# Second attention's keys made behind the last expert slot, routed rows added in one block, 52 unread matmuls ahead of an attention

## What is computed

```python
x = x + tanh(g_xattn[0]) * _L0_xattn_ref(_layernorm(x), ctx, ctx, ...)          # sigmoid attention
x = x + tanh(g_ffn[0])   * _L0_ffn_ref(_layernorm(x), Wr, br, W1, b1, W2, ...)  # 8 experts, three layers, gelu
x = x + tanh(g_xattn[1]) * _L1_xattn_ref(_layernorm(x), ctx, ctx, mask, ...)    # softmax attention
x = x + tanh(g_ffn[1])   * _L1_ffn_ref(_layernorm(x), gate_w, w1, b1, ...)      # 2 experts and a shared FFN
# inside the attention: k = K @ Wk_w + Wk_b ; v = V @ Wv_w + Wv_b   with K = V = ctx
# inside the last part: return routing_output + shared
```

## Time and profile before

| | before |
|---|---|
| median of 3 runs | 883.76 us (882.13 to 883.86) |
| profiled execution | 884.19 us, of which the span of the core is 882.7 us |
| PE, DVE, ACT, POOL busy | 77%, 58%, 37%, 27% of the span |
| mean granted PE clock | 0.887 of full speed |
| stages, from the first instruction of each | sigmoid attention 0, experts 134.9, softmax attention 465.0, last part 680.1 us |

### The profile page before, as it was taken

One profiled execution on the slowest core, in us unless ns is written; L12 is line 12 of the kernel. 1 busy time (PEld: TensorE's weight loads), 2 busy tenths in 40 slices (PEclk: granted clock), 3 DMA queues, 4 the chain that ended last, 5 costly groups with the idle time before them and its releaser, 6 DMA issues. The chain is left out here.

```text
span 882.7 us, 14792 instructions
## 1 busy us (share of the span) xinstructions
PE 679.5 (77%) x4920; PEld 622.8 (71%) x4921; DVE 514.9 (58%) x1231; ACT 323.4 (37%) x546; POOL 237.1 (27%) x365
## 2 busy tenths in 40 slices
PE   3787952176899989999851666786987989999957
PEld 2456642176899988999850453575877889999947
DVE  5543226555775457744634798885554876555535
ACT  3532410444543345433423245434322523333311
POOL 8443326600000000000006165454000621110340
PEclk9897965688999999999985787987999999999978
DMA  4970002624550015660004001000001611111232
GB/s 155 395 296 1 1 0 78 247 84 151 169 175 24 24 71 196 226 232 24 24 30 138 12 1 48 1 1 1 1 1 41 240 62 48 41 34 45 60 95 71
DMA packets 21125, 78.13 MB, mean 89 GB/s; under 512 B 4193, under 2 KB 8546, under 8 KB 16898
## 3 DMA queue, kind: packets, MB, share of 16 engines
q1 hardware_dynamic: 13922, 56.05, 17.4%
q0 software_dynamic: 7168, 21.63, 8.2%
HBM read 50.94 MB, written 33.03 MB: 95 GB/s over the span
## 5 line engine op out<-in xcount | busy, mean ns | idle before, releaser
L1290 ACT ACTIVATE e_h<-psum,e_be 128x256 f32<-128x256 f32 x144 | 67.6, 474 | 148.7 <-PE psum L52 145.1
L50 PE MATMUL psum<-e_h_hi,e_w_hi 128*128 128x256 f32 x384 | 110.3, 287 | 6.2 <-DVE e_w_lo L1374 5.5
L51 PE MATMUL psum<-e_h_lo,e_w_hi 128*128 128x256 f32 x384 | 107.9, 281 | 0.0
L52 PE MATMUL psum<-e_h_hi,e_w_lo 128*128 128x256 f32 x384 | 107.8, 281 | 0.0
L1366 DVE CAST e_h_hi<-e_h 128x256 fp32r<-128x256 f32 x144 | 43.3, 301 | 89.5 <-ACT e_h L1290 89.3
L1635 ACT ACTIVATE vz<-psum,fb 128x256 f32<-128x256 f32 x112 | 52.6, 475 | 115.1 <-PE psum L52 100.3
L50 PEld LDWEIGHTS psum<-e_h_hi,e_w_hi 128*128 128x128 f32 x384 | 72.3, 188 | 9.6 <-DVE e_w_lo L1374 8.8
L51 PEld LDWEIGHTS psum<-e_h_lo,e_w_hi 128*128 128x128 f32 x384 | 72.4, 188 | 0.0
L52 PEld LDWEIGHTS psum<-e_h_hi,e_w_lo 128*128 128x128 f32 x384 | 72.4, 188 | 0.0
L50 PE MATMUL psum<-e_gT_hi,e_w_hi 128*128 128x256 f32 x192 | 56.1, 292 | 15.2 <-issue 7.3
L1368 DVE TENSOR_TENSOR e_h_lo<-e_h,e_h_hi 128x256 fp32r<-128x256 f32 x144 | 61.2, 425 | 4.9
(11 more groups left out here) (367 smaller groups left out, 2157.5 us busy)
## 6 DMA issues: line engine op xcount, KB each, us to landing
e_w_raw<-in_W SPq DMA_DIRECT2D x18, 1024.0 KB, 6.7
xs<-zeros SPq DMA_DIRECT2D x6, 1024.0 KB, 9.5
ys<-zeros SPq DMA_DIRECT2D x6, 1024.0 KB, 14.4
ys<-e_yo POOLq DMA_DIRECT2D x14, 256.0 KB, 3.1
e_xg<-xs POOLq DMA_DIRECT2D x13, 256.0 KB, 3.1
e_w_raw<-in_W SPq DMA_DIRECT2D x6, 512.0 KB, 8.1
f_w_lo<-fw SPq DMA_DIRECT2D x6, 512.0 KB, 7.6
ys<-x_norm POOLq DMA_DIRECT2D x10, 256.0 KB, 2.5
```

The costliest lines, as they stand in the source:

```text
L50: nc.tensor.matmul(out, wh, xh, start=start, stop=False)
L51: nc.tensor.matmul(out, wh, xl, start=False, stop=False)
L52: return nc.tensor.matmul(out, wl, xh, start=False, stop=stop)
L1290: nc.scalar.activation(h32[:, m % RING], ps[:, HIDDEN_BANKS[m % RING], 0:SLOT], ACT.Gelu, bias=be[:, m:m + 1]).then_inc(gelu_ok, 1)
```

## The change

1. In the sigmoid attention the last of the eight norms is refined by DVE (normalise_on_vector, moved up in the file) and applied by ACT.
2. In the experts' stage the zeros of kz_hi, kz_lo and vz are written by ACT (a copy with scale 0) and not by POOL. The keys and values are made behind the loop, in the buffers of w1_hi, w1_lo and xg. DVE makes the low parts of ctx and of the weights ahead of the last slot's bias (finish), and the rest behind it. The values use other PSUM banks.
3. The second attention opens with 52 matmuls of 512 columns on kz_hi, into a bank that is written again before anyone reads it. ACT runs q_hi(0) ahead of norm_1(1).
4. In the last part unit 6 is an ordinary shared unit. In unit 7 the splits run first, then DVE waits for the gathered rows and adds all 16 tiles in a row, then the shared result.

```diff
-            for q in range(len(NORMS)):
+            for q in range(len(NORMS) - 1):
                 pool.wait_ge(mv_ok, q + 1)
...
+                if s == B:
+                    act.wait_ge(rs_ok, len(NORMS))
+                    for i in range(TB):
+                        t = (B - 1) * TB + i
+                        last = nc.scalar.activation(k["xn"][:, t, :], k["x"][:, t, :], ACT.Identity,
+                                                    bias=ln_shift[:, len(NORMS) - 1, i:i + 1], scale=ln_rstd[:, len(NORMS) - 1, i:i + 1])
+                    last.then_inc(n2_ok, 1)
...
                 dve.wait_ge(mv_ok, q + 1)
+                if q == len(NORMS) - 1:
+                    normalise_on_vector(nc, dve, ln_mv[:, q], last_half[:], last_tmp[:], ln_rstd[:, q], ln_shift[:, q], last_step, 0).then_inc(rs_ok, 1)
...
             act.wait_ge(fb_ld, 32)
+            q_hi(0)
             norm_1(1)
-            q_hi(0)
...
+            for _ in range(52):
+                nc.tensor.matmul(ps[:, 7, :], kz_hi[:, 0, 0, 0:P], kz_hi[:, 0, 0, :], start=True, stop=True)
             input_T(0)
...
-                nc.gpsimd.memset(f32(kz_hi[:]), 0.0).then_inc(kz0, 1)
-                nc.gpsimd.memset(f32(kz_lo[:]), 0.0).then_inc(kz0, 1)
-                nc.gpsimd.memset(vz[:], 0.0).then_inc(vz0, 1)
...
+            none = k["ident"][:, None, :]
+            for t in (kz_hi, kz_lo):
+                flat = t[:].rearrange("p b c n -> p (b c n)").rearrange("p (a n) -> p a n", n=P)
+                nc.scalar.activation(flat, none.to_broadcast([P, B * C * HPC * KEYS // P, P]), ACT.Copy, scale=0.0).then_inc(kz0, 1)
...
             visits = dve.value_load(meta[0:1, E0:E0 + 1], min_val=1, max_val=E0)
+            nc.vector.tensor_reduce(odd[:], k["head_rows"][:].rearrange("p (j a) -> p a j", a=2), AX.X, ALU.add).then_inc(odd_ok, 1)
+            dve.wait_ge(ctxh_ok, 1)
...
             finish(n1, visits + 1)
+            dve.wait_ge(odd_ok, 1)
+            dve.wait_ge(kz0, 2)
...
-                sp.wait_ge(x_ok, (b + 1) * TB)
+                sp.wait_ge(x_ok, (b + 1) * TB + b // (B - 1))
...
-            for u in range(DONE + PB, UNITS - PB):
+            for u in range(DONE + PB, UNITS):
                 hidden(u - DONE + n1)
-                for t in range(HALVES):
-                    add_shared(u - DONE + n1, t, k["x"][:, u * HALVES + t, :])
...
+                if u == UNITS - 1:
+
+                    dve.wait_ge(got, 16 * NT)
+                    dve.wait_ge(y_used, (UNITS - DONE - 1 + n1) * HALVES + 2)
+                    for t in range(NT):
+                        add_routed(t).then_inc(x_ok, 1)
+                    dve.wait_ge(x_ok, NT)
                 for t in range(HALVES):
                     add_shared(u - DONE + n1, t, k["x"][:, u * HALVES + t, :])
```

More of the change, by code:

```diff
@@ L70, in normalise, with normalise_on_vector, link @@
     return nc.gpsimd.tensor_scalar(shift, shift, -1.0, None, ALU.mult), count
+def normalise_on_vector(nc, dve, mv, half, tmp, rstd, shift, step, q):
+    count = 10 * q
+    def link(ins):
+        nonlocal count
+        count += 1
+        ins.then_inc(step, 1)
+        dve.wait_ge(step, count)
+    link(nc.vector.tensor_scalar(half, mv[:, :, 1], EPS, -0.5, ALU.add, ALU.mult))
+    for _ in range(3):
+        link(nc.vector.tensor_tensor(tmp, rstd, rstd, ALU.mult))
+        link(nc.vector.tensor_tensor(tmp, tmp, half, ALU.mult))
+        link(nc.vector.scalar_tensor_tensor(out=rstd, in0=tmp, scalar=1.5, in1=rstd, op0=ALU.add, op1=ALU.mult))
+    return nc.vector.scalar_tensor_tensor(out=shift, in0=mv[:, :, 0], scalar=-1.0, in1=rstd, op0=ALU.mult, op1=ALU.mult)
 def sigmoid_attention(nc, k, io):
@@ L505, in _ @@
                     project(s)
[L508 to L523, removed]
 def softmax_attention(nc, k, io):
@@ L1308, in _ @@
             act.sem_inc(gelu_ok, RING)
[L1309 to L1320, removed]
-            for j in range(QUADS):
-                for a in range(2):
-                    r = slice(2 * HD * j, 2 * HD * (j + 1))
-                    nc.scalar.activation(of_head(kz_hi, j, a), of_rows(j), ACT.Copy, scale=odd[r, a:a + 1]).then_inc(kzh_ok, 1)
+            none = k["ident"][:, None, :]
+            for t in (kz_hi, kz_lo):
+                flat = t[:].rearrange("p b c n -> p (b c n)").rearrange("p (a n) -> p a n", n=P)
+                nc.scalar.activation(flat, none.to_broadcast([P, B * C * HPC * KEYS // P, P]), ACT.Copy, scale=0.0).then_inc(kz0, 1)
+            flat = vz[:].rearrange("p b j d -> p (b j d)").rearrange("p (a n) -> p a n", n=P)
+            nc.scalar.activation(flat, none.to_broadcast([P, B * PAIRS * 2 * HD // P, P]), ACT.Copy, scale=0.0).then_inc(vz0, 1)
             act.wait_ge(zero_ok, 1)
@@ L1345, in _ @@
                 act.end_ifs()
+            nc.scalar.activation(ctx_hi, k["ctx_raw"][:, :, :, None, :].to_broadcast([P, C, B, 2, KEYS]), ACT.Copy).then_inc(ctxh_ok, 1)
+            for w in range(2):
+                nc.scalar.activation(kw_hi[:, w], k["w_raw"][:, w], ACT.Copy).then_inc(kwh_ok, 1)
+            act.wait_ge(kp_done, 1)
+            act.wait_ge(kb_ld, 32)
+            for m in range(C):
+                last = nc.scalar.activation(kT[:, :, m, :], ps[:, 2 + m, 0:B * KEYS].rearrange("p (b n) -> p b n", b=B), ACT.Identity,
+                                            bias=bk[:, m:m + 1])
+            last.then_inc(kT_ok, 1)
+            act.wait_ge(kT_ok, 1)
+            act.wait_ge(odd_ok, 1)
+            for j in range(QUADS):
+                for a in range(2):
+                    r = slice(2 * HD * j, 2 * HD * (j + 1))
+                    nc.scalar.activation(of_head(kz_hi, j, a), of_rows(j), ACT.Copy, scale=odd[r, a:a + 1]).then_inc(kzh_ok, 1)
         @block.vector
@@ L1509, in _ @@
                 pe.end_ifs()
+            pe.wait_ge(gelu_ok, n1 * BL + RING)
+            pe.wait_ge(gl_ok, n1 + 1)
+            pe.wait_ge(ctxl_ok, 1)
+            pe.wait_ge(kwl_ok, 1)
+            for m in range(C):
+                for c in range(C):
+                    w = slice(m * P, (m + 1) * P)
+                    last = mm3(nc, ps[:, 2 + m, 0:B * KEYS], kw_hi[:, 0, c, w], kw_lo[:, 0, c, w],
+                               ctx_hi[:, c, :, 0, :], ctx_lo[:, c, :, 0, :], c == 0, c == C - 1)
+            last.then_inc(kp_done, 1)
+            pe.wait_ge(kwl_ok, 2)
+            for b in range(B):
+                for c in range(C):
+                    last = mm3(nc, ps[:, VALUE_BANKS[b], 0:D], ctx_hi[:, c, b].rearrange("p t n -> p (t n)"),
+                               ctx_lo[:, c, b].rearrange("p t n -> p (t n)"), kw_hi[:, 1, c, :], kw_lo[:, 1, c, :], c == 0, c == C - 1)
+                last.then_inc(vp_done, 1)
 def last_ffn_phase(nc, k, io, out):
@@ L1752, in _ @@
             dve.wait_ge(y_used, (UNITS - DONE + n1) * HALVES + 2)
-            dve.sem_inc(x_ok, TB)
+            dve.sem_inc(x_ok, 1)
         @block.tensor
```

82 lines of the change are left out of this document (29 added, 53 removed).

## The result

| | before | changed |
|---|---|---|
| median, the runs of the result (4 and 4) | 883.81 us (882.13 to 886.02) | 861.37 us (859.30 to 863.89) |
| ratio, 95% interval | | 0.9746 (0.9712 to 0.9780) |
| profiled execution, span | 884.19, 882.7 | 860.92, 859.4 |
| granted clock, PE busy | 0.887, 77% | 0.907, 80% |
| last part, from its first instruction to the end | 202.6 us | 188.0 us |

The prediction said 860.6. The last row is why the number must not be carried off alone: on chip 4 the changed kernel is worth nothing. The chip of the first runs is not on record.

What follows compares the result with a forecast made beforehand. The prediction took five stretches where PE waits for chains of small operations as what could move; six differences summed to -23.2 us, giving 860.6 us against the median 883.76, range 855.6 to 866.7.

Steps and rivals of the forecast that it cites:

- last norm: End of the sigmoid attention: the last norm on DVE and ACT takes 4.30 us, not POOL's 6.55; -2.3 us.
- fills leave POOL: Experts' stage: without POOL's fills a held DVE operation takes 0.17 us, not 6.95, so the scatter comes earlier; -6.8 us.
- scatter: Experts' stage: scatter pieces stretch less without keys and values made beside them; -1.6 us, bounds 0 and -2.8.
- keys behind the loop: End of the experts' stage: keys and values, formerly free under the scatter, now delay the stage's end; +6.8 us.
- opening of the softmax attention: Second attention's start: transposes at full clock and query rounded ahead of batch 1's norm bring scores sooner; -4.3 us.
- last part: Shared units 5 to 7: unit 6 follows at once, the wait for gathered rows is covered, 16 additions take 6.5; -15.0 us.
- With q_hi(0) ahead, it is rounded before DVE has ended the norm: Softmax attention's opening: q_lo(0) then follows the norm at once and scores start at 491.4; part of the -4.3 us.
- the 52 matmuls do not help: Rival, softmax attention's opening: the clock level is not kept up, only the reordering gains; 1.5 dearer, 862.1 us; chance 0.12.
- The slower rival (a low clock in units 5 to 7): Rival, last part: PE held at the lower clock, 9.2 us more per unit, 27.6 in all; 888.2 us; chance 0.04.

Runs made afterwards that it cites:

- The last row: The unaltered changed kernel timed again beside the kernel before on chip 4: 887.87 us against 887.40 us, ratio 1.0015 (0.9995 to 1.0035).

## Why the prediction was right, and how far

Step by step on the traces of the result (shifts of the same instruction between the two):

| step | said | measured |
|---|---|---|
| last norm | -2.3 | -2.3 (4.29 against 6.55) |
| fills leave POOL | -6.8 | -7.0 |
| scatter | -1.6 | -2.7, and -1.0 for the wait behind it |
| keys behind the loop | +6.8 | +6.8 |
| opening of the softmax attention | -4.3 | -2.3 |
| last part | -15.0 | -14.6 |
| not forecast | 0 | -1.6 ahead of the last norm, +1.3 around the first slot |
| sum | -23.2 | -23.3 |

**The total is partly luck.** Two terms were off by 2 us each, in opposite directions, and two small things were not in it. The sigmoid attention came to its last norm 1.6 us sooner, in code that the change does not touch; over the traces of all runs that place lies between 117.6 and 121.2 us, so this lies within the spread between executions. Around the first slot 1.3 us were given back, most of it by PE's clock: the slot's first 27 or so matmuls ran 0.21 apart, before 16 or so, and then 0.12. Those two cancel as well. The measured sum holds for the two traced executions.

**Fills.** The reading that POOL's fills held DVE's operation was right. ACT wrote the zeros in 8.1 us, where I had 11.2, under cover in either case.

**Scatter.** I took a little over half of the 2.8 for the keys. It was all of it: the pieces ran at 0.96 with only the first at 1.06, although the splits of the first expert's weights stayed. Beside such splits two pieces had taken 1.48 and 1.50 before and take 0.96 now; why is open. The run with the keys put back shows the same 2.75 from the other side. The landing wait, which I left out, fell from 2.77 to 1.74.

**Keys behind the loop.** From leaving the loop to the next stage 15.4 us, before 8.6 (counted from its last additions). PE starts 2.2 behind the loop, for which I took 2.0, and the last value is written 12.9 later, as said. The drain is under the values, as said, and the values set the end.

**Opening.** The step that failed is "With q_hi(0) ahead, it is rounded before DVE has ended the norm". It needed the query to keep up. The gain of the transposes (0.9 us) was taken by ACT, which had two weight roundings in front (474.25 + 1.99 = 476.24; the copy at 476.15). Then PE, after 1.45 us and 2.96 us of idle time with 1.1 us of transposes between, ran the query at the lower level for all 12 matmuls, 5.5 us; before, the level rose after nine. The 12 matmuls put into the second of these two idle times ran at the full clock, so by that run the level fell in the second and not in the first. The copy came at 484.05, just as DVE's norm ended, and q_lo 1.42 later, not at once. So the scores came at +28.38, where the sum had +26.3. The experiments say what the remaining 2.3 are made of: some 2 are the order (scores at +28.54 without the 52 and at +30.64 before, 2.1; 1.84 between old and new order with the 52), and 0.2 or nothing the 52 matmuls. The rival "the 52 matmuls do not help" was right in its outcome for this place, and not in its reason: the transposes did run at the full clock.

**Last part.** Mechanism and size were right in the trace in which no signal was held. Gathers beside splits took 1.09 (four of them), the last 1.14; the rows were there at the last split, and the additions took 6.4 us for 6.5. The slower rival (a low clock in units 5 to 7) did not come: the granted clock is full up to 848.

**What no step had** is that work moved under a gather depends on signals while the gather runs. Before waits there in any case, so it loses 3 to 4 us where they are held; the changed kernel put unit 6 under the gathers and 52 matmuls ahead of a signal under another gather, and loses 26. The first trace of before could not show it: in it no signal is late. Its trace from chip 9 shows it.

**What stays open** is why the signals are held in every trace of chips 4, 9 and 12 and not in those of the result; with one chip unnamed and the runs made at other times, the chip itself is not shown to be the cause. Incomplete landing records are found in every trace with held signals. Records are lost without a signal being late, too: without the 52 matmuls, ACT copies the transposed rows at once, and the record of the signal that it waited for is missing. Every execution here has records, so it is not shown whether the recording or the DMAs themselves hold the signals; no kernel was timed without records. The Trainium skill (NOTIFIC — Programmer's Manual, section 2.4, When the ring fills) says that a full queue of records, as it is set, loses new records, loses the oldest or stalls the engine; no run here shows which, if any, it was. That the order of the rows in memory, which the plain DMAs also change, has a part, was not tried apart. Nor was it tried how few matmuls in the opening are free of it: with 52 it holds, with none it does not.

## What to carry to other kernels

Work moved under a row gather is only as good as the signals that it needs during the gather: run the changed program on more than one chip, and keep for that place work with few hand-overs between engines. Unread matmuls to raise the clock pay only if the next engine is ready for what they speed up and no idle time follows before the long run; here they were worth 0.2 us at most and cost 6 where signals were held. And a step that is free under another one (the keys under the scatter) should not be moved to save what it disturbs there before both are counted: 3.2 us against 6.3.

## What the runs showed of the hardware

- Under 16 indirect DMAs of POOL in a row (each 128 rows of 1 KB) PE's signals came 7 to 15 us late in the trace from chip 4, while PE went on computing; under 16 plain DMAs of the same bytes none was late.
- POOL's fills of 128x4096 held one DVE instruction until the last fill ended: for 6.95 us a TENSOR_SCALAR of 128x8, for 8.28 us a CAST of 128x128, whichever met them. In the trace of before, a scan, a TENSOR_TENSOR of two SBUF inputs (0.23 us) and a reduce ran beside the first fill unhindered. What was held has one source and goes from SBUF to SBUF; so does the reduce (0.22 us), which was not. The Trainium skill (VectorE: DVE Perf Modes, What auto-detection actually checks) says that such an instruction can take a mode that uses both ports; by that, both held ones qualify. The Trainium skill (GPSIMD Engine Reference, section 8, Key points) names two SBUF inputs as a case of contention as well; the two-input operation beside the fill shows none.
- The other way round, POOL was the slower one: its first scatter piece took 1.83 us and 1.82 (keys under the scatter) beside DVE's subtractions with two SBUF inputs (128x1024, then 128x512), and 1.06 without them.
- ACT fills 128x4096 with zeros in 3.6 us, POOL in 3.5, but nobody stood for ACT's.
- The same ticks of the attention took 184.4 us at a mean clock of 0.88 and 190.9 at 0.81, with the same instructions.
